# A graph kernel on one core: a square moved ahead of the logarithm, a weight fetch one step up its queue, and one copy moved behind an exponential

## The reference, cut to what matters

```
diff = (adj[..., None] - mean_relation) ** 2                 # 4 kernels
w    = exp(-0.5 * diff / (1e-14 + precision_relation ** 2))
w    = w / sum(w, over the 4 kernels)                        # per entry of adj
ws   = sum(w, over a row of adj)
x1   = layernorm(x + concat_k(ws[..., k] * (x @ W0[k].T)))
top1 = argmax(mean(x1, rows) @ router_w + router_b)          # one expert per batch
out  = adj @ (x1 @ expert_w[top1])
y    = relu(batchnorm over rows and batches of the same expert (out)) 
res  = layernorm(x1 + y)
```

## Time and profile before

| | us |
|---|---|
| median of three runs | 885.05 |
| profiled execution, its own time | 887.86 |
| span of its trace | 886.1 |
| PE busy | 753.0 (85%) |
| DVE busy | 755.4 (85%) |
| ACT busy | 766.9 (87%) |
| POOL busy | 687.7 (78%) |

### The profile page before, as it was taken

One profiled execution on the slowest core, in us unless ns is written; L12 is line 12 of the kernel. 1 busy time (PEld: TensorE's weight loads), 2 busy tenths in 40 slices (PEclk: granted clock), 3 DMA queues, 4 the chain that ended last, 5 costly groups with the idle time before them and its releaser, 6 DMA issues.

```text
span 886.1 us, 12505 instructions
## 1 busy us (share of the span) xinstructions
PE 753.0 (85%) x3922; PEld 349.8 (39%) x3922; DVE 755.4 (85%) x1643; ACT 766.9 (87%) x774; POOL 687.7 (78%) x772
## 2 busy tenths in 40 slices
PE   1444469799999999999999999999999999997661
PEld 1111124344444444444444444444444444445440
DVE  2999988699999999999999999999999992227994
ACT  6999998799999999999999999999999961116983
POOL 6699999988888888888888888888888622004794
PEclk9966679999999999999999999999999999998996
DMA  8799886977797779778977797779787728229999
GB/s 231 210 270 261 190 238 166 225 183 192 193 240 193 193 192 239 193 192 195 242 193 190 196 240 192 193 182 249 191 190 168 153 86 330 95 83 392 348 383 359
DMA packets 263925, 191.71 MB, mean 216 GB/s; under 512 B 210098, under 2 KB 210098, under 8 KB 262322
## 3 DMA queue, kind: packets, MB, share of 16 engines
q1 hardware_dynamic: 263714, 190.90, 79.7%
q10 hardware_dynamic: 144, 0.00, 0.0%
HBM read 91.78 MB, written 48.76 MB: 159 GB/s over the span
## 4 chain that ended last, share of the span: by engine, by line
ACT 35%; DVE 26%; POOL 19%; PE 12%; issue 4%; DMA 2%; SPq 0%; POOLq 0%; DVEq 0%; ACTq 0%
DVE ps_t L967 19%; ACT wgt L654 12%; PE ps_z L1136 6%; ACT ps_t L663 6%; ACT ps_t L665 5%; ACT adj_in L648 5%; ACT ps_t L659 5%; POOL adj_cut L512 3%; DVE x_in L951 3%; PE ps_o L1154 3%; DVE wgt L929 3%; POOL x_turn L523 2%; POOL adj_in L507 2%; PE ps_t L1154 2%; POOL adj_cut L510 2%
## 5 line engine op out<-in xcount | busy, mean ns | idle before, releaser
L1136 PE MATMUL ps_z<-adjT,x1p 128*128 128x512 f16 x1536 | 341.3, 379 | 0.0
L1122 PE MATMUL ps_h<-w0T,x_turn 128*128 128x512 f16 x768 | 194.4, 407 | 74.8 <-DVE x_in L951 65.0
L967 DVE TENSOR_TENSOR ps_t<-ps_t,wgt 128x1024 f32<-128x1024 f32 x192 | 234.9, 1224 | 19.0 <-ACT ps_t L659 17.8
L929 DVE SCALAR_TENSOR_TENSOR wgt<-wgt,ps_t 128x1024 f32<-128x1024 f32 x192 | 224.7, 1214 | 15.8 <-ACT ps_t L665 15.8
L1136 PEld LDWEIGHTS ps_z<-adjT,x1p 128*128 128x128 f16 x1536 | 150.2, 98 | 180.5
L648 ACT ACTIVATE wgt<-adj_in,neg_mu 128x1024 f32<-128x1024 f32 x192 | 205.6, 1134 | 7.5 <-POOL neg_mu L567 7.4
L654 ACT ACTIVATE wgt<-wgt 128x3072 f32<-128x3072 f32 x64 | 176.5, 2757 | 0.0
L1154 PE MATMUL ps_o<-zT,w_sel 128*128 128x512 f16 x696 | 161.2, 382 | 4.9 <-DMA w_sel<-w_planes 4.1
L1122 PEld LDWEIGHTS ps_h<-w0T,x_turn 128*128 128x128 f16 x768 | 74.9, 103 | 184.7 <-issue 107.1
L512 POOL TENSOR_TENSOR adj_cut<-adj_in,adj_cut 128x1024 f16<-128x1024 f32 x64 | 136.6, 2134 | 5.3
L1154 PEld LDWEIGHTS ps_o<-zT,w_sel 128*128 128x128 f16 x696 | 68.3, 98 | 88.2 <-DMA w_sel<-w_planes 4.6
(11 more groups left out here) (221 smaller groups left out, 778.2 us busy)
## 6 DMA issues: line engine op xcount, KB each, us to landing
adj_in<-in_adj_dram SPq DMA_DIRECT2D x64, 512.0 KB, 4.0
x_in<-in_x_dram SPq DMA_DIRECT2D x64, 256.0 KB, 4.3
x_spill<-x_in SPq DMA_DIRECT2D x28, 512.0 KB, 3.4
out_spill<-o_stage SPq DMA_DIRECT2D x50, 256.0 KB, 3.1
w_sel<-w_planes SPq DMA_DIRECT2D x8, 1024.0 KB, 8.0
adjT<-x_spill SPq DMA_DIRECT2D x6, 1024.0 KB, 10.2
out_dram<-adjT SPq DMA_DIRECT2D x5, 1024.0 KB, 7.8
adjT<-out_spill SPq DMA_DIRECT2D x4, 1024.0 KB, 12.5
```

The lines of the kernel that those rows point to most:

```text
L929: v.scalar_tensor_tensor(out=wgt[:, m % 2, j, :], in0=wgt[:, m % 2, j, :], scalar=SUM_SCALE / W0_SCALE, in1=tot, op0=ALU.mult, op1=ALU.mul ...
L967: v.tensor_tensor(tot, tot, wgt[:, n % 2, j, :], ALU.add).then_inc(dve_tot, 1)
L1122: last = te.matmul(ps_h[:, n % 2, :], xT[:, n % 2, left, c, :], w0T[:, right, c, :], start=(c + i == 0), stop=(c == C - 1 and i == 2))
L1136: last = te.matmul(ps_z[:, u % 2, :], x1p[:, b % 2, left, t, k * P:(k + 1) * P], adjT[:, b % 2, right, t, half * HALF:(half + 1) * HALF], ...
```

## The change

There are three edits.

1. ACT: the wait for `pool_al` and the solo square of tile n move from behind the wide exponential to ahead of `sum_reciprocal(n - 1)`. `weigh_solo(n)` and its wait stay behind the wide exponential.
2. SP: the fetch of the expert, with its waits, moves from step 13 + 8m to step 12 + 8m.
3. ACT and DVE: of the two z units of step 11 the second (unit 2) is copied behind the wide exponential of the next ACT iteration, and DVE's `low_z(2)` moves one iteration later. Every other step has one z unit or none, and keeps its place.

```diff
+        def z_halves(n):
+            return z_unit(n)[:1], z_unit(n)[1:]
...
-                if u % T == 0 and 0 <= u < TILES:
-                    m = u // T
+                if (u + 1) % T == 0 and 0 <= u + 1 < TILES:
+                    m = (u + 1) // T
...
                     sp.wait_ge(dve_route, m + 1)
-                    wait(sp, pe_o, u)
-                    if u == 0:
+                    wait(sp, pe_o, u + 1)
+                    if m == 0:
                         sp.wait_ge(planes_stored, 16 * E)
                     e = sp.value_load(sc_int[0:1, m % 2:m % 2 + 1], min_val=0, max_val=E - 1)
                     sp.dma_start(w_sel[:], w_planes[e]).then_inc(w_landed, 16)
...
-            def take_z(n):
-                for u in z_unit(n):
+            def take_z(units):
+                for u in units:
...
                 if z_taken_first(n - 1):
-                    take_z(n - 1)
+                    take_z(z_halves(n - 1)[0])
                 take_o(n - 1)
                 if not z_taken_first(n - 1):
-                    take_z(n - 1)
+                    take_z(z_halves(n - 1)[0])
+                if n < TILES:
+                    act.wait_ge(pool_al, n + 1)
+                    if n == 0:
+                        load_spread(SOLO)
+                    square(n, SOLO, adj_in[:, n % ADJ_RING, :])
                 if 0 <= n - 1 < TILES:
                     sum_reciprocal(n - 1)
                 if n < TILES:
                     weigh_others(n)
-                    act.wait_ge(pool_al, n + 1)
-                    if n == 0:
-                        load_spread(SOLO)
-                    square(n, SOLO, adj_in[:, n % ADJ_RING, :])
+                    take_z(z_halves(n - 1)[1])
                     weigh_solo(n)
...
-                    for u in z_unit(n - 1):
+                    for u in (*z_halves(n - 2)[1], *z_halves(n - 1)[0]):
                         low_z(u)
```

## The result

The changed kernel took 928.1 us (median of four runs, 927.76 to 928.71) against 884.77 for the kernel before (median of four, 884.14 to 885.08): a ratio of 1.0489, 95% interval 1.0476 to 1.0503, 43.3 us slower. The forecast was 930.0, range 922 to 940. The profiled execution has a span of 926.4 and an own time of 928.21.

The account below looks back on a forecast made before the run. ACT was taken as the bound, DVE close behind. Steady tiles 44.1 + 0.6 - 0.6, fill 5.5 + 0.8, unit 2 -1.1 and first fetch -4.4 gave +44.9 us, added to the median 885.05: 930 us, range 922 to 940.

Parts of the forecast that it names:

- The wait that binds: Steady tiles: solo exponential still waits for DVE's third row sum, leaving ACT idle about 0.95 us per tile.
- R: End of sum_reciprocal's Exp in a tile, which releases DVE's row sums; the prediction counts times from it.
- Rival A: Solo exponential's wait does not bind, ACT stays without gaps: 876 us, chance 0.04.
- The size per tile: Steady tiles: +1.04 square, -0.10 earlier solo exponential, -0.04 pause; sum +0.90 us, a period of 11.86 us.
- the square ahead of the Ln: Steady tiles: the moved solo square costs its full step there, +1.04 us, and hides nothing.
- the pause: ACT's idle time between z copy and Ln in a steady tile, taken to go: -0.04 us.
- Fill and drain: Start to tile 14: +0.8 us in all, +5.5 of it from tiles 1 to 8; behind the last tile -0.6.
- The first fetch: Tile 14: issued earlier, it ends ACT's 5.32 us stall; -4.4 us in the sum, bounds -5.3 and +0.9.
- The steady fetches: Six early expert fetches fit narrowly into SP's queue: 0, bounds 0 and +2 us each.
- Rival B: Blocked queue delays PE or ACT by 1.5 to 2 us per batch: 940 us, chance 0.13.
- Rival C: PE's clock falls because its gap per tile grows to 1.1 us: over 1000 us, chance 0.02.
- Rival D: Only part of the loss shows, 0.75 us a tile, as the square overlaps its neighbours more: 922 us, chance 0.08.

Follow-up runs that it names:

- the second profile of before: The kernel before, unchanged, profiled a second time: 884.36 us, span 882.6 us.
- edit 2 alone: The kernel before with only the expert's fetch one step up: 884.11 us, ratio 1.0001.
- edits 2 and 3: The kernel before with the earlier fetch and unit 2 copied behind the wide exponential, without edit 1: 884.78 us, ratio 0.9999.
- both attempts at a better version: From tile 14 solo square ahead, next square behind wide exponential: first, with unit 2 and first fetch moved, 889.85 us; second, kernel before, ahead of copies, 880.21 us.
- the two in-place runs: Solo exponential written into adj_in, DVE's first add reading it there: 928.8 us on the changed kernel, 916.0 us on the kernel before.

## Why the prediction was right, and where its sizes were off

**The wait that binds.** Right. R + 3.64 for R + 3.63, an idle time of 0.97 us for 0.95 (62.3 us in all for some 55), and no wait of the Ln for the adds in the steady stage. Rival A falls with it. ACT held the next squares behind the waiting instruction in every tile, as the prediction took from tile 7.

**The size per tile, +0.81 for +0.90.** The term that was too large is the square ahead of the Ln, together with the pause. From the start of the z copy to the start of the Ln it was 0.62 us before (403.85 to 404.47) and is 1.51 now (420.75 to 422.26): +0.89, not 1.04 - 0.04 = 1.00. The pause ahead of the Ln had been read as the time from the copy's end to the Ln's start, 0.04 us. But an ACT instruction that waits for nothing starts some 0.1 us before the one ahead of it ends (o copy 420.27 + 0.57 = 420.84, z copy 420.75). The true wait was 0.04 + 0.1. (Of the 5.6 us that the prediction puts down to the sum, give 3.4 to it; nothing hangs on that.) That is 5 us over 49 tiles. The run with the solo square ahead of the copies shows the same from the other side: a tile without either wait takes 10.86, 0.10 less than before.

**Fill and drain.** The sum was right (+0.57 for +0.8, -0.37 for -0.6), most parts too: tile 12 became 1.25 us shorter (forecast 1.1), tile 14 4.51 shorter (4.4), tiles 9 and 10 0.1 shorter each (0), tiles 11 and 13 0.3 longer each (0.4). Tiles 1 to 8 became 6.2 us longer, not 5.5: the two with late row sums gave back 0.9, as taken, but tile 5 alone took 1.5 more, which was not looked into.

**The first fetch.** Right for the profiled execution, wrong as a term added to the median. Against the second profile of before, tile 14 is only 1.0 us shorter, the fill as a whole is 4.4 us longer and the span 43.8. So two errors of some 4 us met: too much per tile, and a stall that the executions near the median, as far as the second profile stands for them, do not pay in full. The median came out 1.9 us from the forecast partly by that luck.

**The steady fetches, 0.** Right: no period differs near them. SP stood 11.2 us a batch for the ten forecast, though 7.6 of them at another wait first, on the changed count `wait(sp, pe_o, u + 1)`, one more o unit than before. In the trace this wait (the helper `wait`, L46) comes ahead of the one for the routing:

```profile
SPq L460 <- DVE hot_row L894: 50.0, 8, 18.6
...
SPq L46 <- PE ps_o L1160: 45.7, 6, 7.6
```

The cover was not as thin as the prediction had it. It said that without edit 1's slower tiles the fetches might cost something; in the runs of edit 2 alone and of edits 2 and 3 the six fetches cost nothing either. The one place where a wait for POOL reached a period, at the second batch in three runs with a faster fill (edits 2 and 3 together and both attempts at a better version), lies ahead of the first steady fetch and comes from the fill, as shown above. Rival B falls.

**Clock and cover.** PE's granted clock stayed 1.00 over the steady stage with gaps of 0.5 to 1.4 us ahead of its h products. Rival C falls, but not by the argument against it: that the h product behind 2.35 us of idle time ran at full clock held for the profile it was read from, and not for the run of edit 2 alone (4.44 us). Rival D is nearly what came, by its number, 0.81 a tile, and in part by its reason. The chances of B, C, D and the forecast add up to 0.96; the prediction writes 0.95 for slower.

## What to carry to other kernels

Before an instruction is moved forward on a full engine, look at what stood behind it in the old place: it may have been covering a wait that no row shows, because it ended just in time (here 0.16 us before). The loss can be bought back by giving that place other work that is ready, here the next tile's first square; this gave 35 of 43 us back, and applied to the steady tiles alone, with the copies kept late in the period, it beat the original by 3.9 us. A one-off stall in the profile should be seen in a second profile before its whole length enters a sum. And a gain early in the run can be lost at the next place where another engine, here POOL, has no time to spare.

## What the runs showed of the hardware

- A DVE add of 128x1024 float32 with one input in PSUM and one in SBUF took 1217 ns (1215 to 1233). With both inputs in SBUF it had a median of 1484 ns and reached 2679, and POOL's subtraction, 2.13 to 2.15 us before, took up to 3.12. POOL's busy time rose by 54 and 57 us in the two in-place runs (a share of it may be from ScalarE's store into SBUF, which was not separated).
- The length of one stall of PE did not tell which clock followed. Behind stalls of 4.08, 3.39 and 3.00 us, 12 matmuls took 4.25, 4.38 and 4.37 us at a granted clock of about half, 1.2 GHz. Behind 2.35 us they took 2.75 us at full clock, 2.4 GHz, in both profiles of the kernel before and 4.44 us in the run of edit 2 alone. Behind two waits of 0.91 and 1.87 us they took 4.44, behind one of 2.04 us 2.76.
- On ScalarE a dependent exponential starts 1.17 us behind its square (409.08 to 410.25), an independent instruction behind a square 1.04 us (three of them from 400.26 to 403.37): 0.13 us can be had by putting other work between the two.
